# Keys and values of the second attention computed in the attention's own block, with GpSimd drains at three block ends

## The chip, the cores and the metric

One NeuronCore of one Trainium2 chip. The metric is device time in microseconds (us), lower is better. Below, PE is TensorE's matmuls, PEld its weight loads, DVE is VectorE, ACT is ScalarE, POOL is GpSimd, SP is SyncE, which only starts transfers here.

## The reference

Two layers over x (4 batches of 512 rows, 256 wide) with a context of 64 rows per batch. What matters is the passage from the first layer's experts to the second layer's attention:

```python
x = x + tanh(g_xattn[0]) * _L0_xattn_ref(_layernorm(x), ctx_1024, ctx_1024, ...)   # sigmoid attention
x = x + tanh(g_ffn[0]) * _L0_ffn_ref(_layernorm(x), ...)                           # top-1 of 8 experts
x = x + tanh(g_xattn[1]) * _L1_xattn_ref(_layernorm(x), ctx_1024, ctx_1024, mask, ...)   # below
x = x + tanh(g_ffn[1]) * _L1_ffn_ref(_layernorm(x), ...)                           # top-1 of 2, and a shared one

# _L1_xattn_ref, 16 heads of 16
q = Q @ Wq_w + Wq_b;  k = K @ Wk_w + Wk_b;  v = V @ Wv_w + Wv_b
attn = softmax(where(mask == 0, -1e9, q @ k.T / 4), axis=-1)
return (attn @ v) @ Wo_w + Wo_b
```

K and V are both the context, so k and v need nothing that the experts compute. Only the query needs their result.

## The kernel before, in words

The kernel is four blocks, one after the other: `sigmoid_attention`, `experts_phase`, `softmax_attention` and `last_ffn_phase`. Each block holds one list of instructions per engine, written by hand and run in that order; engines meet only at semaphores. At a block's end all engines meet in a barrier. With `no_gpsimd_drain=True`, as in all four blocks before, ACT, PE, DVE and SP drain there (wait for their own instructions to finish) and POOL doesn't. All matrix products take float32 operands split in a high and a low part, three matmuls each (`mm3`, L50 to L52): ACT usually rounds the high part, and DVE subtracts it to get the low one.

`experts_phase` walks through slots of 256 rows, gathered by expert. A slot is 8 first-layer tiles, 4 second-layer tiles and a third product; `finish` (L1546, DVE) adds the bias to the previous slot's result in `yo`, and POOL then writes `yo` to the table `ys` in HBM. After the last slot the same block makes the keys and values of the second attention:

- ACT rounds the context (L1517) and the key and value weights (L1519); DVE takes the low parts (L1640, L1645) and after them calls `finish(n1, ...)` for the last slot.
- PE multiplies keys, 12 matmuls, and then values, 24 matmuls.
- ACT adds the key bias (L1523) and spreads the keys into a table with one head per column block, `kz_hi`, 8 instructions (L1531); DVE makes `kz_lo`, 8 instructions (L1653), and then adds the value bias into `vz`, 8 instructions (L1662).
- POOL writes the last `yo` (L1460), waits for every such store to have landed (L1461), and goes to the barrier (L1304).

`softmax_attention` begins with gathers: POOL starts 16 indirect transfers from `ys`, four per batch (L752). On arrival of a batch `norm_1` on DVE adds it to x (L877) and takes the layer-norm statistics (L859 to L88). ACT applies them (L776), PE transposes (L1011), ACT and DVE split the transposed rows into `xT_hi` and `xT_lo` (L787, L884), PE projects the query, ACT and DVE split that (L794, L890), and PE computes scores. A loop of 27 ticks follows, one 128-row tile in each: DVE clamps the scores (L898) and takes the maxima (L904), POOL subtracts and multiplies, ACT exponentiates, PE transposes and multiplies. In the opening, DVE does the layer norm of batch 1 while PE projects batch 0's query; in the loop it does that of batch b+2 in tick 4b.

Of the kernel before, what the change touches and what calls it, by code (L numbers as in the profile page):

```python
# [10 lines left out]
ALU = mybir.AluOpType  # L11
# [4 lines left out]
KEYS = 64  # L16
# [654 lines left out]
def softmax_attention(nc, k, io):  # L671
# [11 lines left out]
    with ctx:  # L683
# [43 lines left out]
        ps = k["ps"]  # L727
        CLD = 16 * 3
# [42 lines left out]
        def _(act):  # L771
# [83 lines left out]
        def _(dve):  # L855
# [148 lines left out]
        def _(pe):  # L1004
# [35 lines left out]
            def probs_T(n):  # L1040
                pe.wait_ge(nm_ok, n + 1)
# [257 lines left out]
def experts_phase(nc, k, io):  # L1299
# [4 lines left out]
    with ctx:  # L1304
# [3 lines left out]
        def sem(name):  # L1308
# [43 lines left out]
        QUADS = PAIRS // C

        def of_head(t, j, a):
            h = 2 * j + a
            return t[2 * HD * j:2 * HD * (j + 1), :, :, h * KEYS:(h + 1) * KEYS].rearrange("p b c n -> p (b c) n")

        def of_rows(j):
            return kT[2 * HD * j:2 * HD * (j + 1)].rearrange("p b c n -> p (b c) n")

# [17 lines left out]
        block = ctx.enter_context(nc.Block(no_gpsimd_drain=True))  # L1378

        @block.sync  # L1380
        def _(sp):
            sp.dma_start(b12[:], io["b12"]).then_inc(b_ld, 16)
            sp.dma_start(bk[:], io["bk"]).then_inc(kb_ld, 16)
            sp.dma_start(bv[:], io["bv"]).then_inc(kb_ld, 16)
# [79 lines left out]
        def _(act):  # L1464
# [25 lines left out]
            for t in (kz_hi, kz_lo):  # L1490
                flat = t[:].rearrange("p b c n -> p (b c n)").rearrange("p (a n) -> p a n", n=P)
                nc.scalar.activation(flat, none.to_broadcast([P, B * C * HPC * KEYS // P, P]), ACT.Copy, scale=0.0).then_inc(kz0, 1)
            flat = vz[:].rearrange("p b j d -> p (b j d)").rearrange("p (a n) -> p a n", n=P)
            nc.scalar.activation(flat, none.to_broadcast([P, B * PAIRS * 2 * HD // P, P]), ACT.Copy, scale=0.0).then_inc(vz0, 1)
# [21 lines left out]

            nc.scalar.activation(ctx_hi, k["ctx_raw"][:, :, :, None, :].to_broadcast([P, C, B, 2, KEYS]), ACT.Copy).then_inc(ctxh_ok, 1)  # L1517
# [625 lines left out]
```

## Time and profile before

| | us |
|---|---|
| median of 3 runs (840.08 to 844.6) | 841.33 |
| profiled execution, its own time | 842.84 |
| its span, first to last instruction | 841.4 |
| PE busy / PEld busy | 673.5 / 618.4 |
| DVE busy | 523.6 |
| ACT busy | 337.0 |
| POOL busy | 207.0 |

The two slices of the page in which PE falls to 1 tenth of busy time, at about 400 to 440 us, are where the experts end and the second attention opens. A timeline row gives the start, the length of the whole merged group, the line and the tiles, and in brackets how long the engine had been idle and what released it. Rows whose engine ends in q are of the engine's sequencer (branches, semaphores, drains), which count as no busy time.

### The profile page before, as it was taken

What the parts mean: (1) busy time and instruction counts of PE and PEld (TensorE: products, weight loads), DVE (VectorE), ACT (ScalarE), POOL (GpSimd) and SP (SyncE); (2) the same over time, 40 slices, a digit from 0 to 9 for tenths busy, and PEclk for the clock granted to TensorE, in tenths of its full rate; (3) what the DMA queues carried; (4) which work ended last, traced back from release to release, by engine and by line L of the source; (5) the groups of instructions that cost most, each with busy time, mean ns of one, the idle gap of its engine ahead of it and who ended that gap; (6) DMA issues with size and microseconds to landing.
All of it is one profiled execution on the core that took longest, in us unless ns stands there. A gap on an engine that the chain in (4) does not pass through costs nothing. (4 is left out here: it accounts for less than half of the span.)

```text
span 841.4 us, 15063 instructions
## 1 busy us (share of the span) xinstructions
PE 673.5 (80%) x4947; PEld 618.4 (73%) x4948; DVE 523.6 (62%) x1322; ACT 337.0 (40%) x555; POOL 207.0 (25%) x324
## 2 busy tenths in 40 slices
PE   3798925989999999999416667859897799999946
PEld 3566624889999889998414545748797799999946
DVE  6855544776445784448558988865647655655426
ACT  7533344554334552235423454353233323433211
POOL 7522251000000000000071754640004400111340
PEclk9999856999999999999758979879998899999969
DMA  7999126655100559100040010000007201111122
GB/s 257 416 417 393 56 74 254 200 162 181 49 25 25 172 155 372 62 25 19 13 151 6 1 50 1 1 1 1 1 1 263 82 16 48 51 50 41 57 64 100
DMA packets 22997, 90.71 MB, mean 108 GB/s; under 512 B 4401, under 2 KB 8754, under 8 KB 17362
## 3 DMA queue, kind: packets, MB, share of 16 engines
q1 hardware_dynamic: 15794, 68.64, 22.1%
q0 software_dynamic: 7168, 21.63, 8.5%
q8 instruction: 18, 0.29, 0.1%
q14 instruction: 17, 0.14, 0.0%
HBM read 50.94 MB, written 45.61 MB: 115 GB/s over the span
## 5 line engine op out<-in xcount | busy, mean ns | idle before, releaser
L1469 ACT ACTIVATE e_h<-psum,e_be 128x256 f32<-128x256 f32 x144 | 67.7, 475 | 142.2 <-PE psum L52 140.6
L50 PE MATMUL psum<-e_h_hi,e_w_hi 128*128 128x256 f32 x384 | 110.3, 287 | 6.1 <-DVE e_w_lo L1560 5.5
L51 PE MATMUL psum<-e_h_lo,e_w_hi 128*128 128x256 f32 x384 | 107.9, 281 | 0.0
L52 PE MATMUL psum<-e_h_hi,e_w_lo 128*128 128x256 f32 x384 | 107.8, 281 | 0.0
L1863 ACT ACTIVATE vz<-psum,fb 128x256 f32<-128x256 f32 x112 | 52.5, 475 | 119.4 <-PE psum L52 95.9
L1552 DVE CAST e_h_hi<-e_h 128x256 fp32r<-128x256 f32 x144 | 43.4, 301 | 83.1 <-ACT e_h L1469 83.1
L50 PEld LDWEIGHTS psum<-e_h_hi,e_w_hi 128*128 128x128 f32 x384 | 72.3, 188 | 9.6 <-DVE e_w_lo L1560 8.8
L51 PEld LDWEIGHTS psum<-e_h_lo,e_w_hi 128*128 128x128 f32 x384 | 72.4, 188 | 0.0
L52 PEld LDWEIGHTS psum<-e_h_hi,e_w_lo 128*128 128x128 f32 x384 | 72.4, 188 | 0.0
L1554 DVE TENSOR_TENSOR e_h_lo<-e_h,e_h_hi 128x256 fp32r<-128x256 f32 x144 | 61.3, 425 | 4.9
L50 PE MATMUL psum<-e_gT_hi,e_w_hi 128*128 128x256 f32 x192 | 55.7, 290 | 9.4 <-DVE e_w_lo L1627 7.8
L51 PE MATMUL psum<-e_gT_lo,e_w_hi 128*128 128x256 f32 x192 | 55.0, 287 | 0.0
L52 PE MATMUL psum<-e_gT_hi,e_w_lo 128*128 128x256 f32 x192 | 54.9, 286 | 0.0
L1912 DVE TENSOR_TENSOR f_h_lo<-vz,f_h_hi 128x256 fp32r<-128x256 f32 x112 | 47.6, 425 | 3.8
L50 PE MATMUL psum<-xT_hi,sw_hi 128*128 128x256 f32 (+1 forms) x128 | 39.4, 308 | 12.7 <-issue 8.6
L1910 DVE CAST f_h_hi<-vz 128x256 fp32r<-128x256 f32 x112 | 33.3, 297 | 22.2 <-ACT vz L1863 14.6
L50 PEld LDWEIGHTS psum<-e_gT_hi,e_w_hi 128*128 128x128 f32 x192 | 37.3, 194 | 10.8 <-issue 10.8
L763 POOL TENSOR_TENSOR s_sc<-s_sc,s_top 128x1024 f32<-128x1024 f32 x16 | 30.5, 1904 | 56.6 <-DVE s_top L904 56.4
L50 PE MATMUL psum<-kz_hi,s_qT_hi 128*128 128x256 f32 (+1 forms) x80 | 31.0, 388 | 14.9 <-DVE s_sc L898 11.0
L52 PE MATMUL psum<-f_gT_hi,f_w_lo 128*128 128x256 f32 x144 | 40.2, 279 | 0.0
L50 PE MATMUL psum<-f_gT_hi,f_w_hi 128*128 128x256 f32 x144 | 40.2, 279 | 0.0
L51 PE MATMUL psum<-f_gT_lo,f_w_hi 128*128 128x256 f32 x144 | 40.1, 279 | 0.0
(410 smaller groups left out, 2141.1 us busy)
## 6 DMA issues: line engine op xcount, KB each, us to landing
xs<-zeros SPq DMA_DIRECT2D x18, 1024.0 KB
e_w_raw<-in_W SPq DMA_DIRECT2D x18, 1024.0 KB, 5.2
ys<-zeros SPq DMA_DIRECT2D x6, 1024.0 KB
ys<-e_yo POOLq DMA_DIRECT2D x14, 256.0 KB, 3.5
e_xg<-xs POOLq DMA_DIRECT2D x13, 256.0 KB, 6.7
e_w_raw<-in_W SPq DMA_DIRECT2D x6, 512.0 KB, 8.0
f_w_lo<-fw SPq DMA_DIRECT2D x6, 512.0 KB
ys<-x_norm POOLq DMA_DIRECT2D x10, 256.0 KB, 2.6
```

Of the source, the lines that this page charges most:

```text
L50: nc.tensor.matmul(out, wh, xh, start=start, stop=False)
L51: nc.tensor.matmul(out, wh, xl, start=False, stop=False)
L52: return nc.tensor.matmul(out, wl, xh, start=False, stop=stop)
L763: nc.gpsimd.tensor_tensor(sc[:, n % 3], sc[:, n % 3], top[:, n % 2, :, None].to_broadcast([P, HEADS, KEYS]), ALU.subtract).then_inc(sub_ok, 1)
L1469: nc.scalar.activation(h32[:, m % RING], ps[:, HIDDEN_BANKS[m % RING], 0:SLOT], ACT.Gelu, bias=be[:, m:m + 1]).then_inc(gelu_ok, 1)
L1552: nc.vector.tensor_copy(h_hi[:, m], h32[:, m % RING]).then_inc(hh_ok, 1)
L1554: nc.vector.tensor_tensor(h_lo[:, m], h32[:, m % RING], f32(h_hi[:, m]), ALU.subtract).then_inc(hl_ok, 1)
L1863: nc.scalar.activation(h32[:, m % RING], ps[:, HIDDEN_BANKS[m % RING], 0:SLOT], ACT.Relu, bias=b1[:, f * MH + m:f * MH + m + 1]).then_inc( ...
L1910: nc.vector.tensor_copy(h_hi[:, m], h32[:, m % RING]).then_inc(hh_ok, 1)
L1912: nc.vector.tensor_tensor(h_lo[:, m], h32[:, m % RING], f32(h_hi[:, m]), ALU.subtract).then_inc(hl_ok, 1)
```

## The change

The making of keys and values moves from the end of `experts_phase` to the opening of `softmax_attention`. The temporaries lie in the second half of `xT_hi` and `xT_lo` and in `sc` instead of the experts' weight tiles; the value sums go to banks 4 and 5. The two bias loads (bk, bv) move to the head of SP's list in the attention, before the shared expert's weights. On PE, keys and values come before the first transposes. On ACT, context and weights come first, and the key bias and `kz_hi` come before the first layer norm. On DVE, the low parts come first; `kz_lo` comes after the statistics of batch 0; the split of the transposed rows goes ahead of the eight constants; the query's low part goes ahead of the layer norm of batch 1; and `vz` stands between these two. The last `finish` in the experts follows its loop directly. The blocks `experts_phase`, `softmax_attention` and `last_ffn_phase` are built without `no_gpsimd_drain`, so that POOL drains too at their ends; `sigmoid_attention` keeps it.

```diff
@@ softmax_attention
-        block = ctx.enter_context(nc.Block(no_gpsimd_drain=True))
+        block = ctx.enter_context(nc.Block())
         @block.sync
+            sp.dma_start(bk[:], io["bk"]).then_inc(kb_ld, 16)
+            sp.dma_start(bv[:], io["bv"]).then_inc(kb_ld, 16)
...
         @block.scalar
+            nc.scalar.activation(ctx_hi, k["ctx_raw"][:, :, :, None, :].to_broadcast([P, C, B, 2, KEYS]), ACT.Copy).then_inc(ctxh_ok, 1)
             act.wait_ge(k["wa_ld"], 32)
             for w in range(2):
+                nc.scalar.activation(kw_hi[:, w], w_raw[:, w], ACT.Copy).then_inc(kwh_ok, 1)
+            for w in range(2):
                 nc.scalar.activation(w_hi[:, w], w_raw[:, 2 + w], ACT.Copy).then_inc(wh_ok, 1)
+            act.wait_ge(kp_done, 1)
+            act.wait_ge(kb_ld, 32)
+            for m in range(C):
+                last = nc.scalar.activation(kT[:, :, m, :], ps[:, 2 + m, 0:B * KEYS].rearrange("p (b n) -> p b n", b=B), ACT.Identity,
+                                            bias=bk[:, m:m + 1])
+            last.then_inc(kT_ok, 1)
+            act.wait_ge(kT_ok, 1)
+            act.wait_ge(odd_ok, 1)
+            for j in range(QUADS):
+                for a in range(2):
+                    r = slice(2 * HD * j, 2 * HD * (j + 1))
+                    nc.scalar.activation(of_head(kz_hi, j, a), of_rows(j), ACT.Copy, scale=odd[r, a:a + 1]).then_inc(kzh_ok, 1)
         @block.vector
+            nc.vector.tensor_reduce(odd[:], k["head_rows"][:].rearrange("p (j a) -> p a j", a=2), AX.X, ALU.add).then_inc(odd_ok, 1)
+            dve.wait_ge(ctxh_ok, 1)
+            nc.vector.tensor_tensor(ctx_lo.rearrange("p c b t n -> p (c b) t n"),
+                                    k["ctx_raw"][:].rearrange("p c b n -> p (c b) n")[:, :, None, :].to_broadcast([P, C * B, 2, KEYS]),
+                                    f32(ctx_hi.rearrange("p c b t n -> p (c b) t n")), ALU.subtract).then_inc(ctxl_ok, 1)
+            for w in range(2):
+                dve.wait_ge(kwh_ok, w + 1)
+                nc.vector.tensor_tensor(kw_lo[:, w], w_raw[:, w], f32(kw_hi[:, w]), ALU.subtract).then_inc(kwl_ok, 1)
             norm_1(0)
+            dve.wait_ge(odd_ok, 1)
+            for j in range(QUADS):
+                for a in range(2):
+                    dve.wait_ge(kzh_ok, 2 * j + a + 1)
+                    r = slice(2 * HD * j, 2 * HD * (j + 1))
+                    nc.vector.scalar_tensor_tensor(out=of_head(kz_lo, j, a), in0=of_rows(j), scalar=odd[r, a:a + 1],
+                                                   in1=f32(of_head(kz_hi, j, a)), op0=ALU.mult, op1=ALU.subtract).then_inc(kzl_ok, 1)
+            transposed_lo(0, th1_ok, tl1_ok)
             dve.wait_ge(c_ld, CLD)
             nc.vector.tensor_copy(rw_hi[:], rw[:]).then_inc(cst_ok, 1)
...
             nc.vector.tensor_scalar(cap[:], cap[:], MASKED, None, ALU.add).then_inc(cap_ok, 1)
-            transposed_lo(0, th1_ok, tl1_ok)
-            norm_1(1)
             dve.wait_ge(fb_ld, 32)
             q_lo(0)
+            dve.wait_ge(kb_ld, 32)
+            dve.wait_ge(vp_done, B)
+            for b in range(B):
+                src = value_rows(b).rearrange("p (j a d) -> p j a d", a=2, d=HD)
+                for a in range(2):
+                    r = slice(a * KEYS, (a + 1) * KEYS)
+                    last = nc.vector.tensor_tensor(vz[r, b, :, a * HD:(a + 1) * HD], src[r, :, a, :],
+                                                   bv[r, :].rearrange("p (j a d) -> p j a d", a=2, d=HD)[:, :, a, :], ALU.add)
+                last.then_inc(vz_ok, 1)
+            norm_1(1)
         @block.tensor
+                if n == 0:
+
+                    pe.wait_ge(vz_ok, B)
...
+            pe.wait_ge(ctxl_ok, 1)
+            pe.wait_ge(kwl_ok, 1)
+            for m in range(C):
+                for c in range(C):
+                    w = slice(m * P, (m + 1) * P)
+                    last = mm3(nc, ps[:, 2 + m, 0:B * KEYS], kw_hi[:, 0, c, w], kw_lo[:, 0, c, w],
+                               ctx_hi[:, c, :, 0, :], ctx_lo[:, c, :, 0, :], c == 0, c == C - 1)
+            last.then_inc(kp_done, 1)
+            pe.wait_ge(kwl_ok, 2)
+            for b in range(B):
+                for c in range(C):
+                    last = mm3(nc, value_rows(b), ctx_hi[:, c, b].rearrange("p t n -> p (t n)"),
+                               ctx_lo[:, c, b].rearrange("p t n -> p (t n)"), kw_hi[:, 1, c, :], kw_lo[:, 1, c, :], c == 0, c == C - 1)
+                last.then_inc(vp_done, 1)
             input_T(0)
+
+            pe.wait_ge(kT_ok, 1)
             q_proj(0)
             pe.wait_ge(cst_ok, 6)
+            pe.wait_ge(kzl_ok, 2 * QUADS)
             scores(0)
@@ experts_phase: the same instructions are removed from sync, scalar, vector and tensor; around finish
...
-            for w in range(2):
-                dve.wait_ge(kwh_ok, w + 1)
-                nc.vector.tensor_tensor(kw_lo[:, w], k["w_raw"][:, w], f32(kw_hi[:, w]), ALU.subtract).then_inc(kwl_ok, 1)
             finish(n1, visits + 1)
-            dve.wait_ge(odd_ok, 1)
-            dve.wait_ge(kz0, 2)
...
-        block = ctx.enter_context(nc.Block(no_gpsimd_drain=True))
+        block = ctx.enter_context(nc.Block())
@@ last_ffn_phase
-        block = ctx.enter_context(nc.Block(no_gpsimd_drain=True))
+        block = ctx.enter_context(nc.Block())
```

DVE at the end of the experts, before, from the end of the slot loop to the barrier (`e_w_lo` is where the low parts lie, `e_yo` the last slot's result):

```order
L1638 TENSOR_REDUCE e_odd<-head_rows 128x2
L1640 TENSOR_TENSOR e_w_lo<-ctx_raw,e_w_hi 128x1024
L1645 TENSOR_TENSOR e_w_lo<-w_raw,e_w_hi 128x512 x2
L1542 ISA
L1543 REGISTER_ALU x2
L1543 ISA
L1545 ISA
L1546 TENSOR_TENSOR e_yo<-psum,e_b3e 128x256
L1545 REGISTER_ALU
L1546 TENSOR_TENSOR e_yo<-psum,e_b3e 128x256
L1653 SCALAR_TENSOR_TENSOR kz_lo<-e_xg,e_odd,kz_hi 32x8x64 x8
L1662 TENSOR_TENSOR vz<-psum,e_bv 64x8x16 x8
```

and now, from the load of the loop count to the first instruction of the attention:

```order
L1680 TENSOR_LOAD meta
L1680 ISA x2
L1585 ISA
L1586 REGISTER_ALU x2
L1586 ISA
L1588 ISA
L1589 TENSOR_TENSOR e_yo<-psum,e_b3e 128x256
L1588 REGISTER_ALU
L1589 TENSOR_TENSOR e_yo<-psum,e_b3e 128x256
L1385 UNCONDITIONAL_BRANCH
L891 UNCONDITIONAL_BRANCH
L980 TENSOR_REDUCE s_odd<-head_rows 128x2
```

The stores' source `e_yo` had four instructions ahead of it and sixteen behind it before the barrier; now none of either.

DVE in the attention's opening, before, from the last statistics of batch 0 (`s_ln_shift`) to the layer norm of batch 1 (`x_res`):

```order
L88 SCALAR_TENSOR_TENSOR s_ln_shift<-s_ln_mv,s_ln_rstd 128x4
L948 CAST s_rw_hi<-s_rw 128x4
L949 CAST s_bo_hi<-s_bo 128x256
L950 MEMSET s_cap 128x64
L952 TENSOR_TENSOR s_rw_lo<-s_rw,s_rw_hi 128x4
L953 TENSOR_TENSOR s_bo_lo<-s_bo,s_bo_hi 128x256
L954 CAST s_ones_r<-s_cap 128x128
L956 TENSOR_SCALAR s_cap<-s_mask_i 128x256
L958 TENSOR_SCALAR s_cap<-s_cap 128x256
L884 TENSOR_TENSOR xT_lo<-psum,xT_hi 128x2x512
L877 SCALAR_TENSOR_TENSOR x_res<-x_norm,tg,x_res 128x1024
```

and now, from the same place; after the last row shown, the layer norm of batch 1 begins:

```order
L997 SCALAR_TENSOR_TENSOR kz_lo<-s_sc,s_odd,kz_hi 32x8x64 x8
L921 TENSOR_TENSOR xT_lo<-psum,xT_hi 128x2x512
L1001 CAST s_rw_hi<-s_rw 128x4
L1002 CAST s_bo_hi<-s_bo 128x256
L1003 MEMSET s_cap 128x64
L1005 TENSOR_TENSOR s_rw_lo<-s_rw,s_rw_hi 128x4
L1006 TENSOR_TENSOR s_bo_lo<-s_bo,s_bo_hi 128x256
L1007 CAST s_ones_r<-s_cap 128x128
L1009 TENSOR_SCALAR s_cap<-s_mask_i 128x256
L1011 TENSOR_SCALAR s_cap<-s_cap 128x256
L927 SCALAR_TENSOR_TENSOR s_qT_lo<-psum,s_bq,s_qT_hi 128x512 x2
L1020 TENSOR_TENSOR vz<-psum,s_bv 64x8x16 x8
```

Eight instructions for `kz_lo` now stand before the split `xT_lo`, the constants behind it, and the query's low part and `vz` ahead of the layer norm of batch 1.

Further down on DVE, before, from the last statistics of batch 1 to the split of its transposed rows:

```order
L88 SCALAR_TENSOR_TENSOR s_ln_shift<-s_ln_mv,s_ln_rstd 128x4
L890 SCALAR_TENSOR_TENSOR s_qT_lo<-psum,s_bq,s_qT_hi 128x512 x2
L965 TENSOR_TENSOR sw_lo<-sw_lo,sw_hi 128x1024 x2
L898 SCALAR_TENSOR_TENSOR s_sc<-psum,s_cap 128x1024
L904 TENSOR_REDUCE s_top<-s_sc 128x16
L884 TENSOR_TENSOR xT_lo<-psum,xT_hi 128x2x512
```

and now:

```order
L88 SCALAR_TENSOR_TENSOR s_ln_shift<-s_ln_mv,s_ln_rstd 128x4
L1026 TENSOR_TENSOR sw_lo<-sw_lo,sw_hi 128x1024 x2
L935 SCALAR_TENSOR_TENSOR s_sc<-psum,s_cap 128x1024
L941 TENSOR_REDUCE s_top<-s_sc 128x16
L921 TENSOR_TENSOR xT_lo<-psum,xT_hi 128x2x512
```

The query's low part no longer stands between the statistics of batch 1 and the first clamped scores (`s_sc`); everything else of this piece is as it was.

## Rows read from the trace of the kernel before

**Rows 1.** Windows: stretch, length, busy time (and instructions) of PE, PEld, DVE, ACT, POOL.

```profile
401.94:419.86 17.92, 6.59 (x36) 6.42 (x36) 11.20 (x22) 9.54 (x14) 0.71 (x1) 0.76 0.04 16
...
451.31:500.00 48.69, 32.16 (x152) 22.25 (x151) 42.58 (x78) 21.43 (x27) 25.47 (x13) 0.85 0.01 2
```

**Rows 2.** Queue rows of L1637, then L1542: count, shortest/median/longest ns, first to last start.

```profile
L1637 DVEq SEQ_ASSERT  x1: 23/23/23, 404.3 to 404.3; - x1
...
L1542 DVEq FUSED_REGOPS  x7: 46/46/53, 221.5 to 405.7; - x7
```

**Rows 3.** Timeline of DVE, experts' end: start, length, line, tiles, count, [idle before].

```profile
404.61 1.22 DVE L1640 TENSOR_TENSOR e_w_lo<-ctx_raw,e_w_hi 128x1024 fp32r<-128x1024 f32 x1
405.75 1.28 DVE L1645 TENSOR_TENSOR e_w_lo<-w_raw,e_w_hi 128x512 fp32r<-128x512 f32 x2
406.95 0.75 DVE L1546 TENSOR_TENSOR e_yo<-psum,e_b3e 128x256 f32<-128x256 f32 x2
411.27 5.73 DVE L1653 SCALAR_TENSOR_TENSOR kz_lo<-e_xg,e_odd,kz_hi 32x512 fp32r<-32x512 f32 x8 [3.56 <-ACT kz_hi L1531]
417.03 2.46 DVE L1662 TENSOR_TENSOR vz<-psum,e_bv 64x128 f32<-64x128 f32 x8
```

**Rows 4.** Timeline of POOL: the experts' last store, the first gather.

```profile
408.43 0.71 POOL L1460 DMA_DIRECT2D ys<-e_yo  x1 [11.56 <-DVE e_yo L1546]
420.62 1.51 POOL L752 DMA_INDIRECT x_norm<-ys,pos  x1 [11.48 <-POOLq L1304]
```

**Rows 5.** Queue rows of L1304, the experts block's end.

```profile
L1304 DVEq EVENT_SEMAPHORE  x2: 21/21/21, 419.6 to 419.8; - x2
...
L1304 POOLq COMPARE_BRANCH  x1: 38/38/38, 411.0 to 411.0; - x1
```

**Rows 6.** Queue row of L1440, the one POOL drain of the kernel.

```profile
L1440 POOLq DRAIN  x1: 5097/5097/5097, 119.7 to 119.7; - x1
```

**Rows 7.** Timeline of POOL: the last scatter before that drain ends.

```profile
123.68 0.96 POOL L1438 DMA_INDIRECT xs<-x_norm,pos  x1 [0.30 <-issue]
```

**Rows 8.** Timeline of ACT: the experts' end, the first layer norm of the attention.

```profile
402.23 1.28 ACT L1517 ACT_TABLE_LOAD   x1 [2.58 <-issue]
403.52 1.06 ACT L1517 ACTIVATE e_w_hi<-ctx_raw 128x1024 fp32r<-128x1024 f32 x1
...
409.52 0.84 ACT L1523 ACTIVATE e_xg<-psum,e_bk 128x256 f32<-128x256 f32 x2 [3.90 <-PE psum L52]
410.39 5.40 ACT L1531 ACTIVATE kz_hi<-e_xg,e_odd 32x512 fp32r<-32x512 f32 x8
...
433.50 2.07 ACT L776 ACTIVATE s_xq<-x_res,s_ln_shift,s_ln_rstd 128x256 f32<-128x256 f32 x4 [12.49 <-DVE s_ln_shift L88]
```

**Rows 9.** Timeline of PE: first key matmul, last matmul of two query projections.

```profile
406.58 0.55 PE L50 MATMUL psum<-e_w_hi 128*128 128x256 f32 x1 [4.65 <-DVE e_w_lo L1645]
...
444.83 0.63 PE L52 MATMUL psum<-xT_hi,s_w_lo 128*128 128x512 f32 x1
...
457.68 0.40 PE L52 MATMUL psum<-xT_hi,s_w_lo 128*128 128x512 f32 x1
```

**Rows 10.** Timeline of DVE in the attention's opening.

```profile
438.69 1.23 DVE L884 TENSOR_TENSOR xT_lo<-psum,xT_hi 128x1024 fp32r<-128x1024 f32 x1 [3.39 <-ACT xT_hi L787]
...
446.97 1.41 DVE L890 SCALAR_TENSOR_TENSOR s_qT_lo<-psum,s_bq,s_qT_hi 128x512 fp32r<-128x512 f32 x2 [1.43 <-ACT s_qT_hi L794]
448.30 2.35 DVE L965 TENSOR_TENSOR sw_lo<-sw_lo,sw_hi 128x1024 fp32r<-128x1024 f32 x2
451.31 1.23 DVE L898 SCALAR_TENSOR_TENSOR s_sc<-psum,s_cap 128x1024 f32<-128x1024 f32 x1 [0.67 <-PE psum L52]
...
453.72 1.22 DVE L884 TENSOR_TENSOR xT_lo<-psum,xT_hi 128x1024 fp32r<-128x1024 f32 x1
```

**Rows 11.** Tile x_norm, 419 to 462: count, shortest/median/longest ns, first to last start.

```profile
L752 POOL DMA_INDIRECT x_norm<-ys,pos x16: 942/946/1754, 420.6 to 440.2; - x16
L877 DVE SCALAR_TENSOR_TENSOR x_res<-x_norm,tg,x_res x3: 1276/1284/2003, 427.8 to 454.9; 128x1024 f32<-128x1024 f32 x3
```

More of the change, by code:

```diff
@@ L727, in softmax_attention, with of_head, value_rows, of_rows @@
         ps = k["ps"]
+        kb_ld, ctxh_ok, ctxl_ok, kwh_ok, kwl_ok, kp_done, kT_ok, odd_ok, kzh_ok, kzl_ok, vp_done, vz_ok = (
+            sem(n) for n in ("kb_ld", "ctxh_ok", "ctxl_ok", "kwh_ok", "kwl_ok", "kp_done", "kT_ok", "odd_ok", "kzh_ok", "kzl_ok",
+                             "vp_done", "vz_ok"))
+        bk, bv, odd = sb("bk", [P, C]), sb("bv", [P, D]), sb("odd", [P, 2])
+        QUADS = PAIRS // C
+        ctx_hi, ctx_lo = (k[n][:, 0, T // 2:].rearrange("p (c b t n) -> p c b t n", c=C, b=B, t=2) for n in ("xT_hi", "xT_lo"))
+        kw_hi, kw_lo = (k[n][:, 1, T // 2:].rearrange("p (w c d) -> p w c d", w=2, c=C) for n in ("xT_hi", "xT_lo"))
+        kT = sc[:, 0].rearrange("p h n -> p (h n)")[:, 0:B * C * KEYS].rearrange("p (b c n) -> p b c n", b=B, c=C)
+        def of_head(t, j, a):
+            h = 2 * j + a
+            return t[2 * HD * j:2 * HD * (j + 1), :, :, h * KEYS:(h + 1) * KEYS].rearrange("p b c n -> p (b c) n")
+        def value_rows(b):
+            return ps[:, 4 + b % 2, b // 2 * D:(b // 2 + 1) * D]
+        def of_rows(j):
+            return kT[2 * HD * j:2 * HD * (j + 1)].rearrange("p b c n -> p (b c) n")
         CLD = 16 * 3
         sw1_hi, sw1_lo, sw2_hi, sw2_lo = k["sw1_hi"], k["sw1_lo"], k["sw2_hi"], k["sw2_lo"]
-        block = ctx.enter_context(nc.Block(no_gpsimd_drain=True))
+        block = ctx.enter_context(nc.Block())
         @block.sync
         def _(sp):
+            sp.dma_start(bk[:], io["bk"]).then_inc(kb_ld, 16)
+            sp.dma_start(bv[:], io["bv"]).then_inc(kb_ld, 16)
             for h in range(2):
@@ L1491, in _ @@
                 flat = t[:].rearrange("p b c n -> p (b c n)").rearrange("p (a n) -> p a n", n=P)
-                nc.scalar.activation(flat, none.to_broadcast([P, B * C * HPC * KEYS // P, P]), ACT.Copy, scale=0.0).then_inc(kz0, 1)
+                nc.scalar.activation(flat, none.to_broadcast([P, B * C * HPC * KEYS // P, P]), ACT.Copy, scale=0.0)
             flat = vz[:].rearrange("p b j d -> p (b j d)").rearrange("p (a n) -> p a n", n=P)
-            nc.scalar.activation(flat, none.to_broadcast([P, B * PAIRS * 2 * HD // P, P]), ACT.Copy, scale=0.0).then_inc(vz0, 1)
+            nc.scalar.activation(flat, none.to_broadcast([P, B * PAIRS * 2 * HD // P, P]), ACT.Copy, scale=0.0)
             act.wait_ge(zero_ok, 1)
@@ L1515, in _ @@
                 act.end_ifs()
-            nc.scalar.activation(ctx_hi, k["ctx_raw"][:, :, :, None, :].to_broadcast([P, C, B, 2, KEYS]), ACT.Copy).then_inc(ctxh_ok, 1)
-            for w in range(2):
-                nc.scalar.activation(kw_hi[:, w], k["w_raw"][:, w], ACT.Copy).then_inc(kwh_ok, 1)
-            act.wait_ge(kp_done, 1)
-            act.wait_ge(kb_ld, 32)
-            for m in range(C):
-                last = nc.scalar.activation(kT[:, :, m, :], ps[:, 2 + m, 0:B * KEYS].rearrange("p (b n) -> p b n", b=B), ACT.Identity,
-                                            bias=bk[:, m:m + 1])
-            last.then_inc(kT_ok, 1)
-            act.wait_ge(kT_ok, 1)
-            act.wait_ge(odd_ok, 1)
-            for j in range(QUADS):
-                for a in range(2):
-                    r = slice(2 * HD * j, 2 * HD * (j + 1))
-                    nc.scalar.activation(of_head(kz_hi, j, a), of_rows(j), ACT.Copy, scale=odd[r, a:a + 1]).then_inc(kzh_ok, 1)
         @block.vector
```

56 lines of the change are left out of this document (removed).

## The prediction

> **What bounds the kernel now.** I read the slices of the page first. PE is above 9 tenths in the expert blocks and in the last one, and falls to 1 tenth around 400 to 440 us. The windows say what stands there: from the last expert matmul at 401.94 to the opening of the attention at 419.86, PE works 6.6 of 17.9 us and DVE 11.2 [rows 1]. This is the stretch that the change takes apart. The next thing to know is who sets the pace once the attention's loop has begun: DVE, with 42.6 busy of 48.7 us from 451.31 on [rows 1]. So time won or lost until DVE reaches the loop is carried to the end, and time won on another engine is not.
>
> In the old stretch the chain is DVE's. It comes out of the slot loop at 404.3 [rows 2], makes the low parts, adds the last slot's bias at 406.95, waits for `kz_hi`, and ends `vz` at 419.49 (417.03 + 2.46) [rows 3]. Its semaphore comes at 419.6, and all engines are let go at 419.8 [rows 5]; the first gather starts at 420.62 [rows 4]. Everyone else is earlier. POOL has its store started at 408.43 [rows 4] and sees it landed at 411.0 [rows 5].
>
> **Gain: the block ends earlier.** Without keys and values, DVE goes from 404.3 into `finish`. Its register work began at 405.7 and its first addition at 406.95 after DVE came free [rows 2, 3]; I take 0.5 us for that work, which nothing hides now (bounds 0 and 1.25). The additions take 0.75 [rows 3], so they end at 404.3 + 0.5 + 0.75 = 405.55 instead of 407.70, 2.15 earlier. The last store is what is late next: from DVE's end to POOL seeing it landed took 411.0 - 407.70 = 3.3 us [rows 3 to 5], which gives 408.85. Then comes the new drain. The only POOL drain in the trace starts at 119.7 and lasts 5.1 us, but it waits for four scatters' issue, the last of which ends at 124.64 (123.68 + 0.96) [rows 7]; the drain ends at 124.80 [rows 6], 0.16 after it. POOL has nothing running when it passes the wait at L1461, so I take 0.16; the upper bound is 5.1. The barrier itself took 0.2 to 0.3 from the last arrival [rows 5]. The attention opens at 408.85 + 0.16 + 0.25 = 409.3 against 419.8: 10.5 us earlier. The other two drains come at ends where POOL has long had nothing to do: nothing each, at most 0.2.
>
> **Loss: DVE reaches the loop later in its block.** I count from the opening. Before, batch 0's normalised rows start on ACT at 433.50 [rows 8], +13.7; the split `xT_lo` at +18.9, the query's low part at +27.2, the first clamped scores at +31.5, and the split of batch 1 at +33.9 [rows 10].
>
> 1. ACT now begins with the table load and the context's high part, 1.28 + 1.06 [rows 8], done at +2.4. DVE's low parts, 1.22 + 1.28 [rows 3], end at +5.0, and the attention's own weights at about +6.2; the first batch lands at +8.0 (427.8) [rows 11]. So these are under the gathers and cost nothing. If that cover went, they would cost 2.5.
> 2. The first key matmul came 0.83 after the start of the weights' low parts, and the key bias on ACT 2.94 after that (409.52 - 406.58) [rows 3, 8, 9]: +4.5 and +7.5. Bias and `kz_hi` take 0.87 and 5.40 [rows 8], so ACT is free at +13.8, where it has to be at +13.7 for the layer norm. This fits with no room: each us more here is a us more at the end.
> 3. DVE, done with batch 0's statistics at +13.7, makes `kz_lo`, 5.73 [rows 3], to +19.4. Before, it had 3.39 of idle there and, in the rest of the 5.2 from 433.50 to 438.69, the constants ahead of `xT_lo` [rows 8, 10]. `xT_lo` starts 0.5 late. The constants go behind it, beside PE's query projection, for nothing.
> 4. The query's low part follows 8.3 after `xT_lo` (446.97 - 438.69) [rows 10], at +27.7. Here is what the change gives back: before, DVE did batch 1's layer norm in this wait. Now that stands behind, and DVE idles some 5 us. From +27.7 come the query's low part 1.33, `vz` 2.46 [rows 3], batch 1's layer norm 5.7 (as batch 0's, 433.50 - 427.8 [rows 8, 11]) and the shared weights' low parts 2.35 [rows 10]: the first clamp starts at +39.6 against +31.5, 8.1 late.
> 5. Clamp and maxima take 2.4 to +42.0. From ACT's first normalised row to the split it took 438.69 - 433.50 = 5.2 for batch 0 [rows 8, 10]; batch 1's statistics end at +37.2, so its split starts at +42.4 against +33.9. DVE enters the loop 8.5 late in its block, behind which the list is as before.
>
> The values' 24 matmuls end before PE's transposes and block nothing. **Sum:** -10.5 + 8.5 = -2.0 us. Against the profiled execution, 842.84 (span 841.4), it is 840.8; that execution lies 1.5 above the median 841.33, so for a median I say 839.3.
>
> **A rule against the change.** In the old order no DVE work with two SBUF operands but the attention's weights lay beside the first gathers' issue; now three more us of it do. The rows: POOL's issue of a gather takes 0.95, the longest 1.75 [rows 11], and the first, beside such a DVE instruction, 1.51 [rows 4]; and `x_res` takes 2.00 instead of 1.28 once [rows 11]. Three gathers hit at 0.8 each make the first batch 2.4 late. The Trainium skill (SBUF — State Buffer, Who interferes with whom) says it outright: a DVE instruction with two SBUF inputs shares a read interface with a GpSimd instruction that reads SBUF, and the second to issue waits the first one out. By that rule the gathers would be 2.4 later and the sum +0.4; by the median of the sixteen gathers, 0.946, they would be on time.
>
> **Rivals.**
> - *PE at its higher level, or a shorter wait for the query.* The old projection of batch 0 ran at the 1.2 GHz level (0.63 a matmul), that of batch 1 at 2.4 (0.40) [rows 9]. Before it PE had stood nearly idle since the values; now keys and values run shortly before. If it were granted the higher level, 12 x 0.23 = 2.8 us would come off DVE's idle time: 836.5. Against: between values and projection there remain some 8 us in which PE has only the transposes.
> - *No gain.* The gathers or ACT's chain (point 2) come 2.4 late: 839.3 + 2.4 = 841.7.
> - *Slower: the block's end doesn't move.* If another arrival than DVE's holds the barrier (POOL's drain running long, or a store), the opening stays where it was and only the 8.5 remains: 849.8. It would break even with the opening at 411.3, and be slower by over 0.5% from 415.5 on. For it speaks the single 5.1 us drain [rows 6]; against it, that the drain ended 0.16 after the last instruction, and that it would have to be 6 us long.
> - *The change doesn't do what it says.* The order shows that it does.
>
> **Numbers.** About 0.5% (4.2 us) is what a measurement of this kernel can tell from no change. The forecast of -2.0 has 0.52, of which 0.04 falls beyond -4.2 (the 0.5 of register work hidden, `x_res` at 1.28 where it took 2.00, as DVE meets POOL later); PE's level 0.24, faster; no gain 0.14, within; the late end 0.10, slower. Together faster 0.28, same 0.62, slower 0.10. The range reaches down to 835.0 (PE's level and 1.4 of the small terms) and up to 844.0 (a drain of nearly 5 us).
>
> **What would show it.** In the new profile: POOL's last store at 406.3 instead of 408.4; first gather at about 410.1; the first batch's `x_res` 8.0 after the opening; ACT's `kz_hi` ending within 0.3 of the statistics; `kz_lo` directly ahead of `xT_lo` with no idle between; DVE idle some 5 us before the query's low part; and the first clamp 39.6 after the opening, at about 449, against 451.3. The prediction is wrong if the opening is not 9 to 11 earlier, if the clamp is not 7 to 9 later within the block, or if the time from the first clamp to the end, 841.4 - 451.3 = 390.1 before, changes by over 1.5.

## The result and the profile after

The changed kernel took 853.14 us (median of 4, 849.82 to 855.38) beside 840.96 for the kernel before on the same chip: ratio 1.0146, 95% interval 1.0108 to 1.0184. It is 12 us slower. Repeated on another chip (e12 below), where the kernel before takes 820.05, the ratio is 1.0072 (1.0039 to 1.0105). The forecast of 839.3 was wrong, in sign too. The ratios leave out single executions more than 1.5% above the fastest of their kernel: in e6 two of ten (849.0 and 849.7; with them its median is 0.3% above the kernel before), in e14 one of nine (916.8).

The engines' busy times of the page (the line of before is in the table further up):

```profile
PE 683.0 (80%) x4947; PEld 628.8 (74%) x4948; DVE 524.1 (61%) x1322; ACT 337.3 (40%) x555; POOL 207.2 (24%) x324
```

Each engine has as many instructions as before, and only PE became much busier, by 9.5 us (its weight loads by 10.4). The cores' view says by what: the same matmuls at a lower granted clock (0.909 before).

```profile
core 0: 853.0 us, clock 0.892
```

**The opening.** DVE leaves the slot loop 2.4 earlier than in [rows 2]. That is variation of the earlier blocks: the first gather of the kernel before and of its variants e1, e4, e5, e9 and e15 starts anywhere from 416.9 to 421.4. Queue row of L1680:

```profile
L1680 DVEq SEQ_ASSERT  x1: 23/23/23, 401.9 to 401.9; - x1
```

POOL's timeline and the queue rows of the block's end, L1385, answer to [rows 4, 5]:

```profile
403.92 0.71 POOL L1519 DMA_DIRECT2D ys<-e_yo  x1 [9.36 <-DVE e_yo L1589]
410.52 1.05 POOL L774 DMA_INDIRECT x_norm<-ys,pos  x1 [5.89 <-POOLq L1385]
```

```profile
L1385 POOLq COMPARE_BRANCH  x1: 38/38/38, 406.5 to 406.5; - x1
L1385 POOLq DRAIN  x1: 2852/2852/2852, 406.6 to 406.6; - x1
...
L1385 DVEq EVENT_SEMAPHORE  x1: 21/21/21, 409.7 to 409.7; - x1
```

The store lands at 406.5, 3.3 after DVE's end (402.45 + 0.76), as forecast. Then GpSimd's drain takes 2.85 us with nothing left to wait for, and the block opens at 409.7. From the end of the slot loop that is 7.8 us, against 15.5 before: 7.7 gained instead of 10.5. By the span's own clock the opening came 10.1 earlier (409.7 against 419.8), inside the 9 to 11 that the prediction asked for, but only by luck: 2.4 of it are the earlier blocks.

**The block's head.** DVE's timeline (start, length, line, tiles, count, idle before), for [rows 3, 10]:

```profile
419.86 1.29 DVE L914 SCALAR_TENSOR_TENSOR x_res<-x_norm,tg,x_res 128x1024 f32<-128x1024 f32 x1 [4.05 <-DMA x_norm<-ys,pos]
...
425.63 2.83 DVE L997 SCALAR_TENSOR_TENSOR kz_lo<-s_sc,s_odd,kz_hi 32x512 fp32r<-32x512 f32 x4
429.10 2.87 DVE L997 SCALAR_TENSOR_TENSOR kz_lo<-s_sc,s_odd,kz_hi 32x512 fp32r<-32x512 f32 x4 [0.64 <-issue]
434.54 1.23 DVE L921 TENSOR_TENSOR xT_lo<-psum,xT_hi 128x1024 fp32r<-128x1024 f32 x1 [2.57 <-ACT xT_hi L809]
...
441.95 1.41 DVE L927 SCALAR_TENSOR_TENSOR s_qT_lo<-psum,s_bq,s_qT_hi 128x512 fp32r<-128x512 f32 x2 [4.51 <-ACT s_qT_hi L816]
443.27 2.45 DVE L1020 TENSOR_TENSOR vz<-psum,s_bv 64x128 f32<-64x128 f32 x8
445.75 1.28 DVE L914 SCALAR_TENSOR_TENSOR x_res<-x_norm,tg,x_res 128x1024 f32<-128x1024 f32 x1
...
451.51 2.36 DVE L1026 TENSOR_TENSOR sw_lo<-sw_lo,sw_hi 128x1024 fp32r<-128x1024 f32 x2
453.90 1.22 DVE L935 SCALAR_TENSOR_TENSOR s_sc<-psum,s_cap 128x1024 f32<-128x1024 f32 x1
```

`x_res` comes 10.2 after the opening (8.0 forecast), `xT_lo` waits 2.57 for ACT, `q_lo` 4.51; the first clamp is 44.2 in (39.6 forecast, 31.5 before). ACT's and PE's timelines show who was late for `xT_lo`:

```profile
427.61 1.99 ACT L849 ACTIVATE sw_hi<-sw_lo 128x1024 fp32r<-128x1024 f32 x2
433.49 1.02 ACT L809 ACTIVATE xT_hi<-psum 128x1024 fp32r<-128x1024 f32 x1 [3.89 <-remote]
```

```profile
427.76 1.97 PE L1072 MATMUL psum<-ident,s_xq 128*128 128x128 f32 x8 [7.02 <-ACT s_xq L798]
```

PE's transposes end at 429.73 by the record, but the semaphore's own events show its count at 433.46, and ACT starts 0.03 later. The Trainium skill (Perfetto Trace Analysis, Tensor Engine Instruction) says that the end in a PE row is estimated, not observed. The trace agrees that it can be: of the two, ACT followed the semaphore.

**Behind the first clamp.** The stretch from the start of the loop's last clamp (its sixteenth) to the start of the last addition of a shared unit, a piece of the shared expert's work. Columns are stretch, length, PE busy (matmuls), granted clock, DMA share, GB/s; before, then after:

```profile
552.90:629.90 77.00, 61.83 (x468) 0.91 0.00 1
```

```profile
555.40:641.00 85.60, 71.84 (x467) 0.78 0.00 1
```

8.6 us more for the same matmuls, at 0.78 of the clock instead of 0.91. The account of the 11.7 us between the two spans: the loop starts 2.6 later (-2.4 variation, -7.7 opening, +12.7 in the block), runs 0.1 shorter, the shared units +8.6, the last part +0.6.

The beginning of the stretch shows where the two part. Before, then after, up to the clock's first fall and then to its next rise:

```profile
552.90:561.40 8.50, 3.07 (x25) 1.00 0.00 0
561.40:568.30 6.90, 3.92 (x18) 0.51 0.01 2
```

```profile
555.40:558.80 3.40, 0.84 (x8) 1.00 0.01 2
558.80:572.50 13.70, 9.26 (x43) 0.50 0.00 1
```

Before, the clock stays at its upper level (2.4 GHz) for 8.5 us after the last clamp and then stands at the lower one (1.2 GHz) for 6.9. After, it falls 3.4 us behind the last clamp and stays down for 13.7. Over the whole stretch it is down for 13.7 us before and for 37.5 after.

### The profile page after: what moved, and what is told of

It is laid out like the page before. It is cut to its first block and busy times, and to the rows that moved or that the text cites. A ratio compares the mean times of both kernels' runs of the same rounds, so it can differ in the third digit from the quotient of the medians.

```text
span 853.0 us, 15051 instructions
## 1 busy us (share of the span) xinstructions
PE 683.0 (80%) x4947; PEld 628.8 (74%) x4948; DVE 524.1 (61%) x1322; ACT 337.3 (40%) x555; POOL 207.2 (24%) x324
## 5 line engine op out<-in xcount | busy, mean ns | idle before, releaser
L50 PE MATMUL psum<-xT_hi,sw_hi 128*128 128x256 f32 (+1 forms) x128 | 39.1, 305 | 13.6 <-ACT vz L1863 10.7
L50 PE MATMUL psum<-kz_hi,s_qT_hi 128*128 128x256 f32 (+1 forms) x80 | 34.2, 428 | 14.6 <-DVE s_sc L935 10.6
L1910 DVE CAST f_h_hi<-vz 128x256 fp32r<-128x256 f32 x112 | 33.0, 294 | 19.0 <-ACT vz L1863 15.5
```

Of the source, the lines that this page charges most:

```text
L50: nc.tensor.matmul(out, wh, xh, start=start, stop=False)
L1910: nc.vector.tensor_copy(h_hi[:, m], h32[:, m % RING]).then_inc(hh_ok, 1)
```

## The experiments

Each ran beside the kernel before, and is judged by its ratio to it (95% interval), since chips differ: the part behind the last shared addition takes 208.6 to 214.3 us on some and 189.8 to 191.1 on others, whatever the kernel. "Head" is the time from the first gather to the first clamp (30.7 before, 43.4 after), "tail" the stretch just shown (77.0 and 85.6). The median times of e1 to e8, e16 and e17 stand beside 841 for before, the others beside 820.

**e1, the drains alone.** Diff: `Block(no_gpsimd_drain=True)` to `Block()` in three blocks of the kernel before.

> The kernel before, with the three drains given back and nothing moved. Theory A (the drains cost little beside what the barrier takes anyway): the drain at the experts' end costs up to the 2.85 us that it took in the changed kernel, those at the other two ends lie behind the wait for other engines; the block's last part after loop step 15 takes 80 us as before: 841 + 2 to 3 = 843 to 844. Theory B (POOL's drain at the attention's end or its clearing of the queues is what makes the shared units 8.6 us longer): 851 to 853.

Measured: 841.41, 0.9998 (0.9972 to 1.0024). Head 30.7, tail 77.0. The drain is there, and hidden, since DVE is busy in that block until 420:

```profile
L1304 POOLq DRAIN  x1: 2852/2852/2852, 412.0 to 412.0; - x1
```

2.85 us again. It costs nothing where another engine is the last, and all of it where GpSimd is, which is what the move made of it.

**e2, the move alone.** The changed kernel with `no_gpsimd_drain=True` put back.

> The changed kernel with no drains in the three blocks: keys and values moved alone. Theory A (the 8.6 us in the shared units come with the move, by TensorE's granted clock, and the drain is 2.85 less its barrier): 853.1 - 2.7 = 850 to 851, granted clock in the shared units about 0.79 as in the changed kernel. Theory B (the drains did it): first clamp as late in its block as with drains, but the shared units at 80 us as before: about 842.

Measured: 847.64, 1.0067 (1.0030 to 1.0105). The median hides two groups: five times at 841.9 to 845.2 and five at 850.1 to 854.4. The profiled one is of the second; head 43.2, tail 85.5 at clock 0.78. So the drains don't make the tail long. That the move doesn't always do it either is what the first group suggests; no execution of it was traced.

**e3, the second batch's statistics back ahead of the query's low part.** No drains.

```
             cap ...
+            norm_1(1)
             q_lo(0)
             vz ...
-            norm_1(1)
```

> The changed kernel without drains, and on DVE the second batch's statistics ahead of the query's low part, where the kernel before has them. DVE then idles less before the query's low part, and the first clamp comes 4 to 5 us earlier in its block than in e2: about 39.5 after the opening instead of 44.2. If the time after the first clamp only follows (theory C, the loop step is all DVE's and the rest is fixed), the time is e2 minus 4 to 5. If TensorE's clock in the shared units depends on what stands before (theory A), it is e2 minus 4 to 5 and up to 8.6 more or less.

Measured: 844.05, 1.0034 (1.0006 to 1.0062). Head 35.9, 7.3 less than e2: 4.4 of it DVE's idle time before `q_lo`, and 2.9 its wait for the transposes, which wasn't there this time. Tail 85.6.

**e4, extra DVE work in the kernel before.** Two more makings of the low query, 2.8 us, ahead of the first clamp.

> The kernel before, with 2.7 us of extra DVE work (the query's low part of batch 0 made twice more into the other buffer) ahead of the first clamp, nothing moved and no drain. It brings the loop's start to where the changed kernel has it (about +2.6). If a later loop start alone makes the shared units long by a lower granted clock (theory A'), 841 + 2.7 + 8 = 852; if the shift is only carried on: 841 + 2.7 = 843.7, with the time from first clamp to the end unchanged at 390.

Measured: 844.43, 1.0037 (1.0019 to 1.0056); head 33.8, tail 77.0. A later start is simply carried on here.

So far tail 85.6 went with the move each time. Two theories remained: K, that keys' and values' matmuls in this block cause it; and P, that the place of the loop's start against something outside the kernel decides it. The next four shift the start by another amount, on both sides. The extra work is four subtractions of the identity from itself into a free buffer. They were planned at 1.7 us; in the traces four of them took 1.43 us, three 1.10 and two 0.75:

```
             dve.wait_ge(cap_ok, 2)
+            for m, h in ...:  # four of them
+                nc.vector.tensor_tensor(qT_lo[:, 1, m, ...], two, two, ALU.subtract)
             for n in range(TICKS):
```

**e5, the kernel before with it.**

> The kernel before, with four extra DVE subtractions (128x256, 0.43 us each: 1.7 us) directly ahead of the first clamp; keys and values stay in the experts' block, no drain. Theory P (TensorE's granted level in the shared units hangs on when the loop starts against something that the kernel does not set, and not on where keys and values are made; in the five profiles so far the 3.1 us later start of e4 kept the 77.0 us from last clamp to last shared addition): a start 1.7 later lands where the changed kernel stands, 85.6 us in place of 77.0, so 841.4 + 1.7 + 8.6 = 851.7. Theory K (keys' and values' matmuls in this block make the level low later on): 77.0 stays, 841.4 + 1.7 = 843.1.

Measured: 845.94, 1.0060 (1.0037 to 1.0082). Head 31.3, 0.6 later and not 1.4: 0.67 of it fills the time for which the first clamp had waited for the scores. Tail 80.0: neither number. The level fell without any move of keys and values, though not as far as P had said.

**e6, e3 with it.**

> e3 (keys and values moved, no drains, second batch's statistics before the query's low part) with the same 1.7 us of extra DVE work ahead of the first clamp. Theory P: the later start brings the shared units back to about 77.0 us from last clamp to last shared addition: 844.05 + 1.7 - 8.6 = 837.1, so extra work makes the kernel faster. Theory K: 85.6 stays, 844.05 + 1.7 = 845.8.

Measured: 843.56, 0.9986 (0.9948 to 1.0024), spread from 835.3 to 849.7; the profiled one (838.0) has tail 79.9, e5's within 0.1, with keys and values on the other side of the barrier. The semaphore of the transposes was 1.8 late in it (head 38.5). The three fastest, 835.3 to 835.8 at a mean clock of 0.912 to 0.916, stand where 77.0 would put them (834.8 by the profile of e3), but no trace shows them.

**e7, two other savings on e3:** constants ahead of the first batch, shared weights' low parts in loop step 16.

> e3 with DVE's constants moved ahead of the first batch's statistics (into the idle time before its gathers have landed) and the shared weights' low parts (2.36 us) moved from before the first clamp to loop step 16, where DVE idles 3.3 us. First clamp about 33.5 us after the first gather instead of 35.9. Theory P: the start is 2.4 earlier, and by the same token as in e6 the shared units go back to 77.0 us: 844.05 - 2.4 - 8.6 = 833.0. Theory K: 844.05 - 2.4 = 841.7.

Measured: 841.35, 1.0025 (1.0001 to 1.0050). Missed. The constants waited for their load until 417.0 and held up `x_res`, so the head stayed at 35.8, and the subtraction in step 16 took 4.0 us instead of 2.36 and delayed the split behind it; tail 83.8.

**e8, the changed kernel itself with the four subtractions.**

> The changed kernel itself, drains and order as they are, with the same 1.7 us of extra DVE work ahead of the first clamp. Theory P: 853.1 + 1.7 - 8.6 = 846.2, 77.0 us in the shared units. Theory K: 853.1 + 1.7 = 854.8, 85.6 us.

Measured: 846.18, 1.0059 (1.0034 to 1.0083). The same work added, 1.4 us, and the tail is 77.0: P's number, where K said 85.6.

**e9, the kernel before with the shared weights' low parts in step 16.**

> The kernel before, with one thing changed: the low parts of the shared weights (2.36 us on DVE, ahead of the first clamp) are made in loop step 16 instead, where DVE idles about 3 us. Theory P: the time from last clamp to last shared addition follows when the loop starts; 2.4 earlier leaves the place where it is 77.0, so 80 to 86: 841 - 2.4 + 3 to 9 = 842 to 848, slower in spite of less work ahead of the loop. Theory K (only where keys and values are made matters): 77 stays, 838.6.

Measured: 827.18, 1.0092 (1.0063 to 1.0121), tail 83.9, head 30.7. P's number, and not clean: the head didn't shorten (the first clamp now waited 3.0 us for the scores), while step 16 itself was disturbed as in e7. It suggests that a delay of about 1 us at that place (split 11.3 us after the last clamp, 10.1 before) costs 7 in the tail; in e7, e10 and e11 the split comes 11.3 after it too.

**e10 and e11, the same on e3, without and with 1.1 us of extra work.**

> e3 with the same move of the shared weights' low parts, and the constants left where e3 has them (in e7 they waited for their load until 417.0 and held up the first batch). First clamp 33.5 after the first gather (35.9 in e3). Theory P: somewhere between 77 and 85.6 in the shared units, where no profile has stood yet: 844.05 - 2.4 - 0 to 8.6 = 833 to 841.7. Theory K: 841.7.

> e10 with three extra DVE subtractions (1.3 us) ahead of the first clamp, aimed at the start for which the shared units take 77.0. Theory P: below e10 in spite of the extra work, about 844.05 - 1.1 - 8.6 = 834.4, in those executions in which the wait for the first transposes is short. Theory K: e10 + 1.3.

Measured: 1.0018 (0.9996 to 1.0040) and 1.0003 (0.9979 to 1.0027). Heads 33.4 and 34.6, both tails 84. Both within noise of the kernel before; a dead end.

**e12, the changed kernel again.**

> The changed kernel once more, for its spread and a second profile. In the first one the semaphore of the first batch's transposes came 3.7 us after they had ended. If that is fixed by the program, it is there again (xT_lo 24.0 after the first gather) and the times keep to 850 to 855; if it differs from run to run, some times lie 3 to 4 lower, and where the start of the loop then lands elsewhere, 8 lower again (about 845).

Measured: 826.77; five times at 822.1 to 824.4 (clock 0.911 to 0.921) and five at 829.2 to 831.0 (0.901 to 0.903). Its profile has no late semaphore, head 40.0, and tail 85.5:

```profile
430.54 1.02 ACT L809 ACTIVATE xT_hi<-psum 128x1024 fp32r<-128x1024 f32 x1 [0.17 <-PE psum L1072]
```

So the late semaphore differs from execution to execution, and the head is 40.0 without it. The upper group is 10 us over the kernel before, the lower 3. The clocks suggest that the groups have different tails, but the medians lie 6.6 apart and not 8.6, and only one execution, of the upper group, was traced. Which tail the lower group has is not shown.

**e13, the low parts of the shared weights on GpSimd, which idles then (on e3).**

```
             gather(3)
+            for h in range(2):
+                pool.wait_ge(f1h_ok, h + 1)
+                nc.gpsimd.tensor_tensor(sw1_lo(h), f32(sw1_lo(h)), f32(sw1_hi(h)), ALU.subtract)...
```

> e3 with the low parts of the shared weights (2 x 1.18 us on DVE, ahead of the first clamp) made by GpSimd after its last gather, where it idles for over 15 us; at 1.9 us for 128x1024, as its subtractions in the loop take, 3.8 us. First clamp 33.5 after the first gather (35.9 in e3). Theory P: the loop starts where 77.0 us were seen from last clamp to last shared addition (e4, e8): e3's +0.34% of before, minus 2.4, minus 8.6: about 8 us (1.0%) under the kernel before. Theory K: 85.6 stays, e3 - 2.4: equal to the kernel before (+0.05%).

Measured: 816.66, 0.9962 (0.9948 to 0.9976), tail 77.0, head 38.0. The tail is as P said, the head is not. GpSimd's timeline, then DVE's:

```profile
430.25 4.68 POOL L784 TENSOR_TENSOR sw_lo<-sw_lo,sw_hi 128x1024 fp32r<-128x1024 f32 x2
```

```profile
430.10 1.22 DVE L924 TENSOR_TENSOR xT_lo<-psum,xT_hi 128x1024 fp32r<-128x1024 f32 x1
431.25 3.73 DVE L1004 CAST s_rw_hi<-s_rw 128x4 fp32r<-128x4 f32 x1
434.89 0.28 DVE L1005 CAST s_bo_hi<-s_bo 128x256 fp32r<-128x256 f32 x1
```

A cast that takes 0.16 in e3 took 3.73 and ended with GpSimd's work. The Trainium skill (SBUF — State Buffer, Who interferes with whom) has an exclusive lock between these two engines. The trace agrees: the work saved on DVE was paid there again.

**e14, e3 with 0.75 us of extra work.**

> e3 with two extra DVE subtractions (0.9 us) ahead of the first clamp. Theory P: it lands in the middle of the starts that gave 77.0, so most executions have it: e3 + 0.9 - 8.6, about 5 us (0.6%) under the kernel before. Theory K: e3 + 0.9, 0.45% above it.

Measured: 815.99, 0.9946 (0.9929 to 0.9964). Head 36.4, 0.5 more than e3, tail 77.0. Work added, time lost 7 us: P, and the kernel is faster than the one before. Tails of e14 and, for comparison, of e3 and e8:

```profile
545.20:622.20 77.00, 61.88 (x467) 0.91 0.00 1
```

```profile
543.40:629.00 85.60, 71.82 (x467) 0.78 0.00 1
```

```profile
558.30:635.30 77.00, 61.84 (x467) 0.91 0.00 1
```

**e15, e13's edit on the kernel before.**

> The kernel before with the same work moved to GpSimd, nothing else: 2.4 us less on DVE ahead of the first clamp, and loop step 16 untouched. Theory P: the start leaves the place that gives 77.0; from last clamp to last shared addition 80 to 85.6, so before - 2.4 + 3 to 8.6: 0.1 to 0.7% slower in spite of less work. Theory K, and the plain sum: 77.0 stays, 2.4 us (0.3%) faster.

Measured: 822.87, 1.0039 (1.0019 to 1.0059), but tail 77.0, head 33.0: slower by the head, not by the tail. Here too an operation of DVE ran into GpSimd's work (a 128x4 `TENSOR_SCALAR` of the statistics took 3.68 us, 0.17 elsewhere), and the first clamp waited 3.16 for the scores. P's range of times was hit for the wrong reason, and the tail that P had forecast, 80 to 85.6, didn't come: P as it was put, by the size of the shift, missed here.

**e16 and e17, e14 with and without the three drains, side by side.**

> e14 with the three drains given back. By the profile of the changed kernel (2.85 us in GpSimd's drain at the experts' end, nothing beside it) the opening comes 2.9 later: e14 + 2.9, 0.35% more. Rival: the drain is hidden or taken up by later waits, e14 + 0 to 0.5. With the opening, all of the block moves alike, so its place against the granted clock may change too; then the shared units show it (more than 77.0).

> e14 unchanged, on the same chip as e16: if the 0.54% under the kernel before was no accident of one chip, it is 0.4 to 0.7% under it again, with 77.0 us in the shared units.

Measured: 842.63 (1.0027, 0.9999 to 1.0054) and 837.74 (0.9980, 0.9951 to 1.0008). The medians lie 4.9 us apart and the ratios 0.47% (4.0 us), with intervals of 2.3 us either way on each, where the drain's own 2.85 was expected. The profiled pair has tails of 76.9 and 77.0, and its semaphore was 1.8 late in e16 alone. So the drain's price shows in the time, but its size is known only from its own row. And e14's gain came out smaller here, 0.2% with an interval that reaches over 1.

**e18, where the first batch's 2.4 us went (on e3).** The load of the values' bias is issued last; ACT now waits for the keys' bias alone, and DVE for the values' bias before `vz`.

```
             sp.dma_start(bk[:], io["bk"]).then_inc(kb_ld, 16)
-            sp.dma_start(bv[:], io["bv"]).then_inc(kb_ld, 16)
             ...
             sp.dma_start(k["fb1"][:], io["fb1"]).then_inc(fb_ld, 16)
+            sp.dma_start(bv[:], io["bv"]).then_inc(bv_ld, 16)
```

> e3 with the load of the values' bias (128 KB) issued last on SyncE's queue instead of second; DVE needs it 30 us later. If that load is what holds up the first batch's rows, x_res comes 1 to 2.4 us earlier: 7.1 to 8.6 after the first gather instead of 9.6, and the first clamp 33.5 to 34.9 after it instead of 35.9. Rival: the gathers' issue or the weights' load sets it, x_res stays at 9.6. The time by theory P: an earlier start of the loop by 1 to 2.4 moves towards the starts that gave 77.0, where 8.6 more come off; between 0.25% over (no effect) and 1.0% under the kernel before.

Measured: 813.1 beside 820.35, 0.9917 (0.9900 to 0.9933), 4 times from 810.8 to 813.6: the best of all, and faster than both kernels. DVE and GpSimd:

```profile
413.84 1.33 DVE L915 SCALAR_TENSOR_TENSOR x_res<-x_norm,tg,x_res 128x1024 f32<-128x1024 f32 x1 [2.54 <-DMA x_norm<-ys,pos]
...
440.27 1.23 DVE L936 SCALAR_TENSOR_TENSOR s_sc<-psum,s_cap 128x1024 f32<-128x1024 f32 x1
```

```profile
406.01 1.04 POOL L775 DMA_INDIRECT x_norm<-ys,pos  x1 [3.00 <-POOLq L1386]
```

`x_res` 7.8 after the first gather instead of 9.6, head 34.3, tail 77.0. One load's place in SyncE's queue gave 1.8 us at `x_res`, 1.6 at the loop, and the shift that this made gave 8.6. The window of the tail:

```profile
541.70:618.70 77.00, 61.85 (x467) 0.91 0.00 1
```

## Why the prediction was wrong

By its own steps, for the first profile of the changed kernel:

| step | forecast | measured | |
|---|---|---|---|
| register work and `finish` | 1.25 | 1.27 | held |
| DVE's end to the store landed | 3.3 | 3.3 | held |
| GpSimd's drain | 0.16 | 2.85 | failed, +2.7 |
| barrier | 0.25 | 0.25 | held |
| opening to `x_res` | 8.0 | 10.2 | failed, +2.2 |
| ACT's `kz_hi` done | +13.8 | +13.6 | held |
| gap in `kz_lo` | 0 | 0.64 | not foreseen |
| idle before `xT_lo` | 0 | 2.57 | failed; 0 in e12 |
| `xT_lo` to `q_lo` | 8.3 | 7.4 | 0.9 better |
| `q_lo` to the first clamp | 11.9 | 11.95 | held |
| first clamp to the split of batch 1 | 2.8 | 2.86 | held |
| first clamp to the end | 390.1 | 399.1 | failed, +9.0 |

**The drain.** I read the one drain of the trace [rows 6, 7] as waiting for the last scatter and took the 0.16 behind it; its 5.1 us stood as the upper bound. All five traces that have it at the experts' end show 2.852 us, with no GpSimd work in flight. It was wrong to read from a single row in which wait and fixed price could not be told apart. The late-end rival asked for the same thing but needed 6 us of it to turn the sign.

**The gathers.** I put the later landing down to GpSimd and DVE getting in each other's way, and gave it a rival of 2.4 us. The size was right and the cause wrong: the issues kept their pace (0.95 to 1.16 each, sixteen of them). The two bias loads now stand first in SyncE's queue, at the opening instead of in the experts' block. The description of the change names this, but the prediction had no term for it. The rows of `x_res` in all profiles: 7.1 to 7.2 after the first gather in the kernels with the old place, 9.3 to 10.0 with the new one (e7 apart, where DVE itself was late), 7.8 in e18 with the larger load moved back. What the remaining 0.7 is due to, the small load or something else, no run shows.

**The order on DVE.** The idle time before `q_lo` was forecast (5, measured 4.5) and is the largest thing that the change gives away: with the old order the head falls from 40.0 (e12, no late semaphore) to 35.9 (e3).

**The query's projection.** From `xT_lo` to the query's low part it took 7.4 instead of 8.3, the rival on PE's level in small: the last four of the twelve matmuls ran at the higher level. The prediction priced this at 0.23 us a matmul from the rows' lengths; by their starts, 0.43 apart at the lower level and 0.23 at the higher, it is 0.20, and all twelve would have given 2.4 us, not 2.8.

**What was missing: the tail.** The forecast carried the start of the loop to the end unchanged. In the loop itself that held to within 2 us (100.8 to 102.7 us in all profiles). Behind it PE sets the pace, and there the granted clock was 0.78 instead of 0.91. It is not the drains (e1: 77.0; e2: 85.5 without them), and not the place of keys and values (e8, e14, e18: 77.0 with the move; e5: 80.0 without it). Extra work or less work ahead of the loop switches it: e14 and e8 add 0.75 and 1.4 us of idle arithmetic, and e18 takes 1.6 away, and in all three 8.6 us go.

It isn't the time at which the loop starts, though. The first clamp came at 451.31 in the kernel before, with 77.0, and at 451.30 in e12, with 85.5. What goes with the tail in all twenty traces is where the loop stands against the changes of the granted clock. Behind the last clamp the clock stayed up for another 3.4 us in the four executions with 85.5 (after, e2, e3, e12), for 7.9 in e5 and e6 (80.0) and in e7, and for 8.4 to 8.6 in the other thirteen, which take 77.0 except for e9, e10 and e11 with their late split (83.9). Within the tail the clock was down for 37.5, 20.5 and 13.7 us, and for 27.3 in the four with the late split. A shift ahead of the loop isn't handed on as it is either: e14's first clamp came 0.6 later than e3's and its last one 1.8 later. Theory K is out by e8, e13 and e14. Theory P had the tail right in e8, e13, e14 and e18 and wrong in e5, e6 and e15: it went by the size of the shift, and not by where the clock's changes fall. No run set these changes themselves, so that they are the cause and not only go with it rests on e8, e14 and e18, which changed nothing behind the start of the loop. The Trainium skill (TensorE: Matmul & The Clock Gate, What's actually happening) says that the monitor behind the clock runs freely and isn't reset by a kernel; that equal kernels fall into groups 7 to 9 us apart (e2, e12), and that the same start goes with either tail, agrees with it, but is no proof.

So the cost of the change itself, with a tail of 77.0 and no late semaphore, is 1.6 us at the start of the loop: 7.7 gained up to the opening, 9.3 lost in the block (head 40.0 in e12 against 30.7). The forecast had -2.4 there. The drain's 2.7 and the loads' 2.2, less the 0.9 of the query's projection, make the 4.0 between them. In the profiled pair, 11.7 us apart, the tail adds 8.6, the late semaphore 3.3 and the loop and the last part 0.5; against them stand the 2.4 by which the earlier blocks happened to be shorter.

**Left open:** what delays the transposes' semaphore, by 1.8 to 3.7 us in five of the fourteen traced executions with keys and values in the attention (after, e2, e6, e8, e16) and in none without. No run took it away on purpose.

## What to carry to other kernels

When a change moves code across a barrier, list what each queue then issues first, the load queue above all, and ask which engine now arrives last: a price like the drain's 2.85 us is nothing or all of its length by that alone. Where a PE-bound stretch follows one that another engine paces, time it separately and try the same kernel with a little idle work ahead; a difference of 8 us may hang on 1 us of shift, and must not be credited to the edit under test. And look at the single times, not only at their median: two groups may be two mechanisms.

## What the runs showed of the hardware

- GpSimd's drain with nothing in flight took 2.852 us in each trace that has one at the experts' end. The changed kernel's other two took 3.3 and 17.4 us, hidden behind other engines that worked longer, so the length at one place says nothing of another:

```profile
L683 POOLq DRAIN  x1: 3319/3319/3319, 562.7 to 562.7; - x1
```

```profile
L1747 POOLq DRAIN  x1: 17434/17434/17434, 808.4 to 808.4; - x1
```

- The same 467 matmuls took 77.0, 80.0, 83.9 or 85.6 us with a granted clock of 0.91, 0.87, 0.84 or 0.78, and 0.75 us of extra work ahead made the last into the first (e3, e14). How long the clock stayed up behind the last clamp (8.5, 7.9 or 3.4 us) told 77.0, 80.0 and 85.6 apart in all sixteen traces without the late split.
- The semaphore of PE's last instruction before an idle stretch came up to 3.7 us after the end that its row shows.
- Beside a subtraction of GpSimd a DVE cast of 0.16 us took 3.73 (e13), and a `TENSOR_SCALAR` of 0.17 us took 3.68 (e15).
